# Attention's scattered copies: three transfers of 32 rows for the dense halves, and another order on the sync queue, GpSimd and VectorE

## The reference

```python
h = tok(x)                                  # (32, 188, 256): conv, mean, layernorm
x = layernorm(h)
q = x @ W_q
latent = (x @ W_k + x @ W_v) @ W_down_kv
k_rec, v_rec = latent @ W_up_k, latent @ W_up_v     # 16 heads of 16
scores = q_h @ k_rec_h.T / sqrt(d)                  # (16, 188, 188) per sequence
scores = scores * decay                             # exp(-0.01 |t - s|)
attn = softmax(scores)
h = h + concat(attn @ v_rec_h) @ W_o
h = h + experts_and_shared_ffn(layernorm(h))
```

## Time and profile before

| | |
|---|---|
| median of 3 runs | 2042.38 us |
| profiled execution | its own time 2044.36 us, its span 2042.2 us |
| busy share of the span | PE 85%, PE's weight loads 62%, DVE 60%, ACT 46%, GpSimd 46% |
| granted clock of TensorE, mean | 0.917 of full speed |
| the attention stage | from some 140 us to 975 us of the span |
| the chain that ended last | PE 52%, issue 18%, DMA 15%, GpSimd 6% |
| DMA queues | SP's 145272 packets, GpSimd's 26880 |

### The profile page before, as it was taken

How to read it: one execution, slowest core, us unless ns; L and a number is a source line. 1 busy time by engine, 2 the same in 40 slices (tenths; PEclk the granted TensorE clock), 3 DMA queues, 4 the chain that set the end, 5 groups by cost and what they waited for, 6 DMA issues and landing times.

```text
span 2042.2 us, 47014 instructions
## 1 busy us (share of the span) xinstructions
PE 1732.3 (85%) x15406; PEld 1269.4 (62%) x15406; DVE 1226.7 (60%) x3822; ACT 944.0 (46%) x2157; POOL 945.9 (46%) x945
## 2 busy tenths in 40 slices
PE   6856677777777777776799995999999999999997
PEld 5854445555555555553577773777777777777775
DVE  3883566666666666665857775555555555555551
ACT  3534545455555455543533254444444444444442
POOL 3851233333333333323722232466666666666665
PEclk9985888888898888988899995999999999999999
DMA  5512433333343333332421114233433334444322
GB/s 176 185 61 70 100 96 94 92 99 95 95 103 96 95 94 98 94 92 60 122 47 31 31 28 155 81 95 96 107 104 101 107 93 114 98 97 98 95 31 29
DMA packets 172243, 186.70 MB, mean 91 GB/s; under 512 B 111480, under 2 KB 146808, under 8 KB 166008
## 3 DMA queue, kind: packets, MB, share of 16 engines
q1 hardware_dynamic: 145272, 141.18, 24.3%
q0 software_dynamic: 26880, 44.36, 10.8%
HBM read 134.59 MB, written 50.44 MB: 91 GB/s over the span
## 4 chain that ended last, share of the span: by engine, by line
PE 52%; issue 18%; DMA 15%; POOL 6%; DVE 4%; SPq 2%; ACT 2%; POOLq 0%; DVEq 0%; ACTq 0%
PE psum L1756 24%; PE psum L1773 12%; DMA weighed<-arena 10%; PE psum L1621 6%; PE psum L1641 4%; POOL arena L613 2%; DMA arena<-k_halves 2%; POOL hidden L591 1%; POOL arena L596 1%; SPq L475 1%; DMA arena<-arena 1%; PE psum L1736 1%; DMA inverse_sums<-arena 1%; POOL arena L631 1%; ACT arena L759 1%
## 5 line engine op out<-in xcount | busy, mean ns | idle before, releaser
L1756 PE MATMUL psum<-arena,hidden 128*128 128x376 f16 x3072 | 493.5, 323 | 1.2 <-DVE arena L1369 0.9
L658 POOL TENSOR_TENSOR arena<-arena 128x376 f16<-128x376 f32 x320 | 314.9, 986 | 357.3 <-ACT arena L759 355.9
L1756 PEld LDWEIGHTS psum<-arena,hidden 128*128 128x128 f16 x3072 | 301.0, 98 | 189.6 <-issue 1.8
L808 ACT ACTIVATE arena<-psum 128x376 f32<-128x376 f32 x384 | 184.4, 480 | 308.9 <-PE psum L1462 299.5
L759 ACT ACTIVATE arena<-arena 128x376 f16<-128x376 f32 (+5 forms) x610 | 283.7, 473 | 61.2 <-DVE arena L1305 44.9
L1133 DVE CUSTOM_DVE_ANT_0 arena<-psum,constants 128x188 f32<-128x188 f32 x768 | 236.8, 345 | 86.4 <-PE psum L1448 80.6
L613 POOL TENSOR_TENSOR arena<-arena 128x376 f16<-128x376 f32 x128 | 114.7, 900 | 369.7 <-ACT arena L759 366.6
L977 ACT ACTIVATE arena<-psum 128x376 f32<-128x376 f32 x256 | 123.7, 483 | 342.9 <-PE psum L1756 342.9
L1142 DVE TENSOR_TENSOR psum<-psum,constants 128x376 f32<-128x376 f32 x384 | 212.2, 553 | 112.0 <-PE psum L1474 111.4
L1773 PE MATMUL psum<-hidden,arena 128*128 128x256 f16 (+1 forms) x2304 | 256.6, 273 | 0.0
L759 ACT ACTIVATE arena<-psum 128x188 f32<-128x188 f32 (+7 forms) x457 | 176.2, 398 | 163.6 <-PE psum L1736 58.0
(11 more groups left out here) (158 smaller groups left out, 2747.7 us busy)
## 6 DMA issues: line engine op xcount, KB each, us to landing
arena<-e_g SPq DMA_DIRECT2D x16, 1024.0 KB
arena<-e_u SPq DMA_DIRECT2D x16, 1024.0 KB, 5.0
arena<-e_d SPq DMA_DIRECT2D x16, 1024.0 KB
arena<-x_t SPq DMA_DIRECT2D x32, 376.0 KB, 3.5
weighed<-arena POOLq DMA_DIRECT2D x32, 376.0 KB, 8.8
arena<-q_halves SPq DMA_DIRECT2D x192, 47.0 KB
arena<-k_halves SPq DMA_DIRECT2D x192, 47.0 KB
q_halves<-arena SPq DMA_DIRECT2D x32, 188.0 KB, 5.9
```

The source lines that it names most:

```text
L658: nc.gpsimd.tensor_tensor(dst, f, hi, ALU.subtract).then_inc(ready, 1)
L808: nc.scalar.activation(PT[:, i % 6 * 2 * S:(i % 6 + 1) * 2 * S], TB[i % 3], ACT.Exp).then_inc(exp_done, 1)
L1756: last = mm(bank[2 * (s % 2) + i][:, 0:CHUNK], w_, a, start=n == 0, stop=n == 5)
```

## The change

`read` of a dense tile makes three transfers of 32 rows in place of one of 32 rows and one of 64 rows, whose source was the same 32 rows twice (a leading dimension of size 2 with no stride). The counts that PE waits for go from 128 to 144 a batch, since there are now 9 transfers in place of 8. On SP the write of Q's halves goes ahead of the write of the inverse sums, and the write of K's halves goes in between the write and the read of the inverse sums. On GpSimd `low` of K goes ahead of `dense_heads`. On DVE `invert` goes from step 5 to step 8.

```diff
             def read(blocks, dense, dram, c, single, par, landed):
-                both = 1 - single // 2
                 if blocks is None:
-                    for low, r, n in ((1, single, 1), (0, both, 2)):
-                        src = dram[c, low, :, :, :].rearrange("h (d a) n -> (h d) (a n)", a=HP)
-                        sp.dma_start(dense[par][32 * r:32 * (r + n), :], src.unsqueeze(0).broadcast_to((n, 32, HP * S)) if n > 1 else src).then_inc(landed[par], 16)
+                    for r in range(3):
+                        sp.dma_start(dense[par][32 * r:32 * r + 32, :],
+                                     dram[c, int(r == single), :, :, :].rearrange("h (d a) n -> (h d) (a n)", a=HP)).then_inc(landed[par], 16)
...
                     read(KD, None, k_dram, b + 1, 2, 1 - par, st_in)
+                write(q_dram, b + 3, QS, ql_ready, q_out)
                 c = b - 1
                 if valid(c):
                     sp.wait_ge(sums_inverse, c + 1)
...
-                write(q_dram, b + 3, QS, ql_ready, q_out)
+                write(k_dram, b + 3, KS2, kl_ready, k_out)
                 if valid(c):
                     sp.wait_ge(rs_out, 16 * c + 16)
...
-                write(k_dram, b + 3, KS2, kl_ready, k_out)
...
                 low(QS[:, 2 * S:4 * S], QF, QS[:, 0:2 * S], qh_ready, b + 3, ql_ready)
+                low(KS2[:, 2 * S:4 * S], KF, KS2[:, 0:2 * S], kh_ready, b + 3, kl_ready)
                 dense_heads(b - 1)
-                low(KS2[:, 2 * S:4 * S], KF, KS2[:, 0:2 * S], kh_ready, b + 3, kl_ready)
...
-                    elif n == 5:
+                    elif n == 8:
                         invert(b - 1)
...
-                        pe.wait_ge(s_in[cpar], 64 * c + 128 - 64 * cpar)
+                        pe.wait_ge(s_in[cpar], 72 * c + 144 - 72 * cpar)
...
-                        pe.wait_ge(st_in[cpar], 64 * c + 128 - 64 * cpar)
+                        pe.wait_ge(st_in[cpar], 72 * c + 144 - 72 * cpar)
```

## The result

The changed kernel takes 1892.82 us (median of 4 runs, 1889.73 to 1893.54) beside 2042.82 us for the kernel before: ratio 0.9262, 95% interval 0.9245 to 0.928. Forecast were 1905 us, 1870 to 1975, faster with a chance of 0.91. The profiled execution has a span of 1891.4 us.

What follows compares the result with a forecast made beforehand. No engine was full; PE's waits for late K copies stalled the 24.31 us batch. With the sync queue bounding at 19.6, 28 batches save 131.9 and the fill 5: 137 off 2044.4, 2.0 less for the median, 1905 us (1870 to 1975).

Steps and rivals of the forecast that it cites:

- The mechanism: 64-row transfers with leading dimension 2 run on two of 16 DMA engines and hold up the small writes queued behind.
- The batch afterwards: Time per batch after the change: the sync queue's round, 17.02 us plus the inverses' write-to-read time, 19.6 us.
- L: On the sync queue, time from the write of the inverses to their read: 5.57 us before, taken as 2.6.
- The gap and `KX`: In the sync queue's round, three issues of the K copies, 1.74 us, and a gap of 0.36.
- PE's pace: PE's own time per batch without the stalls, with 1.0 us of lost clock regained: 18.4 us.
- B: Rival: PE is slower than taken, by clock or engines waiting for one another; 20.5 us a batch, 1931 us, chance 0.22.
- K's write into the wait: K's write, issued while the sync queue waits for the inverses, leaves its path: 0.64 us a batch saved.
- Q's write ahead: Q's write before the inverses' write puts 0.86 us on the sync queue's path and 188 KB ahead of them.
- Invert in step 8: DVE's wait of 4.1 us a batch for the sums goes, but the inverses start later against PE.
- Fill and tail: Gain outside the 28 batches: 5 us for the four that fill the pipeline, 0 for the tail.
- Rival A: The split brings nothing and the late invert delays SP: 28.0 us a batch, 103 us more, 2146 us, chance 0.06.
- C: Rival: inverses' write-to-read time stays long, 5.0 us, behind Q's write; SP's round 22.0 us, total 1978 us, chance 0.17.

Runs made afterwards that it cites:

- `split_pad2`: `split_only` with 8 blank rows in DRAM between the two groups of each half, so each 32-row transfer stays 2 x 16 rows; 2115.92 us in one run.
- `wide64`: The changed kernel with each dense tile in one transfer of 64 different rows and one of 32; 1887.45 us, ratio 0.9236.
- `split_qfirst`: `split_only` plus Q's write ahead of the write of the inverse sums; 1879.39 us, ratio 0.9194.
- `split_kearly`: `split_only` plus K's write between the inverses' write and read, and GpSimd's `low` of K ahead of `dense_heads`; 1845.03 us, ratio 0.9034.
- `split_only`: The kernel before with only the three transfers of 32 rows and PE's counts of 144; 1853.40 us, ratio 0.906.
- `reorder_only`: The changed kernel with the old pair of transfers, one of 32 and one of 64 rows; 2058.88 us, ratio 1.0069.
- `split_inv8`: `split_only` plus `invert` in step 8; 1855.59 us, ratio 0.908.
- `inv5`: The changed kernel with `invert` back in step 5; 1889.69 us, ratio 0.9242.

## Why the prediction was right, and where its terms were off

*The mechanism.* Read from a share of 0.13 and late small writes, it holds: `split_pad2` brings the stall, the share and the late write back by the leading dimension alone, `wide64` keeps the 64 rows without them. The split carries the gain: 191 us alone, against 150 for the whole. The forecast has no figure for the split alone, and it counted K's write and the late invert as gains; together the other parts lose 39 us.

*The batch afterwards*, forecast 19.6, measured 19.61, with the sync queue as the bound. It is right as a sum, but three terms were off and cancel; that the two agree to 0.01 us is luck. From 532.05 to 551.85 one round is 19.80. L was taken as 2.6 and is 3.74 (532.05 to 535.79): +1.1. The gap and `KX`, forecast 1.74 + 0.36, are 1.89, and `QX` with its gap is 1.36 and not 1.94: -0.8, since a 32-row issue takes 0.42 to 0.53 and not 0.58. Q's write to the inverses is 0.70 and not 0.86. For L the step with Q's write alone in front (2.5, taken as 2.6) is about what `split_qfirst` has, 2.81. What failed is the step that "`dense_heads` is delayed by nothing unless its data come in under that": they came in 4.1 us after their issue in place of 8.8, GpSimd's read was then issued 3.6 us after them, and it stands with Q's write just ahead of the inverses. L had no term for it.

*PE's pace*, forecast 18.4, is 17.8 in `split_kearly`, where PE no longer waits: the clock at 1.00 gave back more than the 1.0 us that I had taken. So B didn't come.

*K's write into the wait.* "Leaves the path" is right by itself (-8 us) and wrong beside Q's write (+10). The prediction had no term for what one part does to another.

*Q's write ahead*, +0.86 on the path: measured 0.88 a batch, 26 us, of which its issue is 0.70 and the longer L the rest. *Invert in step 8:* the 4.1 us of DVE's wait were indeed gone, but the split alone had already removed them (DVE waits for the sums 0.2 us in 400 in `split_only`); the step itself gained nothing (2 to 3 us slower in each pair).

*Fill and tail.* 5 and 0 us were forecast, 13.5 and 5.6 measured. This and nothing else is the difference between 137 and 151. The filling batches stalled about as long as the others (PE's waits for the K copies from 140 to 229.5 are 13.8 us in four, and with the change, up to 216, 2.1 in two), and I had taken a third of that without a row for it. "The tail reads no dense copies" isn't so either: one for Q is issued at 920.04, behind the 29th write at 910.29, and that round's read of the inverses comes 5.44 us after their write, 2.36 with the change. That is 3.1 of the 5.6.

*Rival A*, sized at +103 us for a split that brings nothing, is what `reorder_only` is: +15 us. The mechanism is there (PE waits 82.4 us in 400), its price was wrong, because L was kept at 5.57 although the write of the inverses moves out of the broadcasts' way. With 2.16 for it the same loop gives 24.6, and 25.03 was measured. *C* had the right place, since L did stay above what I took, but not the size: 5.0 was its L, 3.74 the measured one.

## What to carry to other kernels

When the DMA share of a stretch sits at a small whole number of sixteenths while large packets pass, look at the leading dimension of the transfers in flight, and at who is queued behind them: a small transfer that lands three times later than elsewhere (6.1 us against 1.7 here) is the symptom. Put a queue's long issues and large writes into the gap in which it waits for a small round trip, and issue them behind the small transfer, not ahead of it. When an engine's order changes, look at what transfers it also issues: the read that GpSimd now issued later came to stand ahead of another queue's small write. And price the parts of a change one by one and in pairs: this one took 150 us off, while its first part alone takes 191 off, and one of the others helps or hurts by its neighbour.

## What the runs showed that I hadn't expected

- A gap of 8 rows in DRAM, which moves no byte more, costs 262 us (1853.40 to 2115.92), because it keeps two dimensions from being merged and leaves a leading dimension of 2; the same two dimensions without a gap cost nothing (1888.36 beside 1887.45).
- Three issues of 32 rows of 3008 bytes take 1.25 to 1.6 us, not one and a half times the 1.16 of a 32-row and a 64-row one.
- An 11.8 KB write lands in 1.7 us (`split_kearly`, `split_inv8`, `reorder_only`), 2.5 (`split_only`, `split_qfirst`) or 3.6 to 3.8 (the changed kernel, `inv5`). 188 KB issued 0.7 us behind it on the same queue goes with 1.7 as well as with 3.8; 188 KB issued on GpSimd's queue about 1 us ahead of it go with the later landings.
